# The second network of a macaron block: token tiles in groups of 20 and 12 in place of 16 and 16

## The reference, cut to what matters

```python
def ffn(x):                                   # x: 4096 x 128, 8 experts of hidden width 352
    scores = softmax(x @ gate_w.T)
    sel = top_k(scores + expert_bias, 2)
    # per token: sum over its two experts e, fed with score * x
    #   (silu(xe @ w1[e]) * (xe @ w3[e])) @ w2[e]
x = x + 0.5 * ffn(layernorm(x))               # first network
x = x + attention(layernorm(x))               # 16 heads of width 8, no causal mask
x = x + 0.5 * ffn(layernorm(x))               # second network
```

## Time and profile before

| | us |
|---|---|
| median of three runs | 736.26 |
| the profiled execution | 741.27 |
| its span, first to last instruction | 739.5 |
| first network's loads and routing | about 0 to 237 |
| attention | about 237 to 504 |
| second network's loads | 507 to 688 |
| last 32 result gathers, last sums and stores | 691.65 to 739.5 |

### The profile page before, as it was taken

The page is one execution under the profiler, slowest core; times in us unless marked ns, Lnnn a source line. Parts: engine busy times, 40 slices in busy tenths (PEclk is TensorE's granted clock), DMA queues, the critical chain, the costliest instruction groups (busy, mean ns, idle before and its releaser), DMA issues.

```text
span 739.5 us, 14928 instructions
## 1 busy us (share of the span) xinstructions
PE 622.7 (84%) x5050; PEld 474.7 (64%) x5050; DVE 446.2 (60%) x1164; ACT 390.3 (53%) x912; POOL 302.3 (41%) x312
## 2 busy tenths in 40 slices
PE   6399999999988788999899998898999989999200
PEld 6388899888866334445455554456989979989100
DVE  6956733235456899999999999881576322233111
ACT  1625654445422577777877777773457534444000
POOL 6067614665433273045000010005565057777574
PEclk9999999999999789999999999998999999999655
DMA  8358978887982544445343433035679678887322
GB/s 261 100 164 226 243 219 225 230 249 201 293 235 78 168 143 138 123 137 144 106 149 113 139 107 102 3 111 160 175 221 276 189 194 241 241 256 209 106 78 64
DMA packets 116586, 126.02 MB, mean 170 GB/s; under 512 B 12512, under 2 KB 99168, under 8 KB 116384
## 3 DMA queue, kind: packets, MB, share of 16 engines
q1 hardware_dynamic: 98544, 101.20, 45.6%
q0 software_dynamic: 9088, 18.63, 10.2%
q10 hardware_dynamic: 8880, 5.25, 2.3%
HBM read 89.37 MB, written 35.39 MB: 169 GB/s over the span
## 4 chain that ended last, share of the span: by engine, by line
PE 51%; DVE 24%; DMA 7%; issue 6%; POOL 5%; ACT 4%; SPq 2%; POOLq 0%; ACTq 0%; DVEq 0%
PE banks L684 12%; DVE mx L816 10%; PE banks L656 8%; PE banks L672 8%; PE banks L665 8%; PE banks L1127 4%; POOL rows L588 4%; DMA WR<-in_experts 3%; PE banks L646 2%; PE banks L471 2%; ACT PT L1142 2%; DMA xe<-routed_rows,idx 2%; PE banks L1100 2%; PE banks L1011 2%; DVE resid L803 1%
## 5 line engine op out<-in xcount | busy, mean ns | idle before, releaser
L568 POOL DMA_INDIRECT xe<-routed_rows,idx x156 | 151.0, 968 | 231.5 <-PE banks L646 75.5
L816 DVE TENSOR_REDUCE mx<-banks 128x2 f32<-128x512 f32 x256 | 163.3, 683 | 9.4 <-PE banks L1102 8.1
L1142 ACT ACTIVATE PT<-banks 128x512 f32<-128x512 f32 x256 | 140.5, 603 | 34.5 <-PE banks L1113 32.4
L588 POOL DMA_INDIRECT rows<-slots_out,slot x128 | 123.8, 967 | 69.6 <-issue 27.8
L737 DVE TENSOR_TENSOR hidT<-banks,act 96x256 f32<-96x256 f32 (+1 forms) x92 | 34.9, 380 | 192.3 <-ACT act L718 190.2
L684 PE MATMUL banks<-WR,hidT 128*128 128x128 f32 x936 | 120.6, 276 | 0.6 <-ACT ye L727 0.6
L684 PEld LDWEIGHTS banks<-WR,hidT 128*128 128x128 f32 x936 | 112.6, 192 | 2.9 <-issue 1.0
L656 PE MATMUL banks<-xeT,WR 128*128 128x256 f32 (+1 forms) x368 | 87.0, 359 | 7.2 <-issue 3.0
L672 PE MATMUL banks<-xeT,WR 128*128 128x256 f32 (+1 forms) x368 | 83.7, 350 | 0.0
L665 PE MATMUL banks<-xeT,WR 128*96 128x256 f32 (+1 forms) x368 | 83.2, 349 | 0.0
L1100 PE MATMUL banks<-KS,QS 56*128 56x256 bf16 x256 | 67.9, 283 | 11.6 <-DVE mx L816 9.7
(11 more groups left out here) (160 smaller groups left out, 888.9 us busy)
## 6 DMA issues: line engine op xcount, KB each, us to landing
WR<-in_experts SPq DMA_DIRECT2D x92, 544.0 KB
stacks<-split SPq DMA_DIRECT2D x32, 384.0 KB
slots_out<-ye SPq DMA_DIRECT2D x156, 64.0 KB
QS<-stacks SPq DMA_DIRECT2D x64, 112.0 KB
KS<-stacks SPq DMA_DIRECT2D x64, 112.0 KB
routed_rows<-xn ACTq DMA_DIRECT2D x16, 256.0 KB, 5.1
routed_rows<-xn SPq DMA_DIRECT2D x12, 256.0 KB, 2.3
xe<-routed_rows,idx POOLq DMA_INDIRECT x156, 4.4
```

Of the source, the lines that this page charges most:

```text
L568: eng.indirect_dma_start(xe[:, i % XR, a, :], None, routed_rows[h], bass.IndirectOffsetOnAxis(ap=idx[h][:, tile:tile + 1], axis=0))\
L588: eng.indirect_dma_start(rows[:, k, t, :], None, slots_out[h], bass.IndirectOffsetOnAxis(ap=slot[h][:, k, t:t + 1], axis=0))\
L816: eng.tensor_reduce(mx[:, :, e, pair], maxima_bank(f)[:, :].rearrange("p (q n) -> p q n", q=2), AX.X, ALU.max).then_inc(s_max, 1)
L1142: eng.activation(PT[:, u % 4, 1 - k].rearrange("p t n -> p (t n)"), PS[f % 3], ACT.Exp, scale=scale).then_inc(s_exp2, 1)
```

## The change

`GROUPS = (16, 16, 20, 12)` gives each group its own number of tiles; `FIRST` is its first tile and `LOAD0` its first load. The first network stays at 16 and 16. The second network has 27 + 19 loads in place of 23 + 23; as before 32 pairs and 14 singles. Group 2's loads 21 to 26 are all pairs, and group 3 ends with two singles.

- Routing tensors are sized for 20 tiles and indexed by the group's own size. The constants `count` and the table `there` hold one choice's columns only; `there` is used twice.
- Group 2's routing waits for 10 attention sequences in place of 8. Its statistics have a fifth step. ScalarE and VectorE make 20 tiles of rows each; the fifth block of VectorE lies in two slots of the `xe` ring, which is now `XR` = 11 loads.
- Group 3's routing has tables of its own: `VECTOR_LAST` ends at load 16 where the one before ended at load 19, `SCALAR_LAST` makes the last row by load 15 in place of load 19.
- GpSimd fetches for group 3 from load 21 (3, 2, 2), gathers group 2's 40 results from load 30 (2, 3) beside one fetch a load, and at the end gathers group 3's 24 results in place of 32. The first of these waits for all five sums of group 2, as it reuses their buffers.
- `opening_tensor` has three `keep_pace` products behind each of its five head pairs, 15 in all.

```diff
-XR = 16
+GROUPS = (TH, TH, 20, 12)
+FIRST = (0, TH, 0, GROUPS[2])
+XR = 11
...
-        s_gath = [[sem(f"s_gath{h}_{c}") for c in range(GC)] for h in range(HALVES)]
+        s_gath = [[sem(f"s_gath{g}_{c}") for c in range(t // 4)] for g, t in enumerate(GROUPS)]
...
-            for i in range(KT):
-                if i % (KT // 2) == 0:
-                    eng.wait_ge(s_hot, 6 * g + 3 + 3 * (i // (KT // 2)))
-                last = eng.matmul(PS[7][:, 0:2 * NT].rearrange("p (v j) -> p v j", v=2), hot[:, :, i], brow[:, :, :, i],
-                                  start=i == 0, stop=i == KT - 1)
+            T, K, tiles = GROUPS[g], TOP_K * GROUPS[g], TOP_K * GROUPS[g] + NS
+            for i in range(K):
+                if i % T == 0:
+                    eng.wait_ge(s_hot, 6 * g + 3 + 3 * (i // T))
+                last = eng.matmul(PS[7][:, 0:2 * tiles].rearrange("p (v j) -> p v j", v=2), hot[:, :, i],
+                                  brow[:, :, 0:tiles, i], start=i == 0, stop=i == K - 1)
...
-            for k, c in ((0, 0), (0, 1), (0, 2), (1, 0), (0, 3), (1, 1), (1, 2), (1, 3)):
+            for k, c in ((0, 0), (0, 1), (0, 2), (1, 0), (0, 3), (1, 1), (1, 2), (0, 4), (1, 3), (1, 4)):
...
+        def combined(g, c):
+            return sum(GROUPS[0:g]) // 4 + c + 1
+
+        def combined_before(g, c):
+
+            if 4 * c >= TH:
+                return combined(g, c - TH // 4)
+            return combined(g - 1, max(range(c, GROUPS[g - 1] // 4, TH // 4))) if g > 0 and GROUPS[g - 1] > 4 * c else \
+                combined(g - 2, c) if g > 1 else 0
...
             for pair in range(5):
                 for e in range(2):
                     for _ in largest_scores(eng, (1, pair), e):
...
+                keep_pace(eng, 3, PS[0])
...
-            outs = expert_gpsimd(pool, 2, 6, spread((0, 17, 2)),
-                                 spread((16, NL + 3, 3, 3, 2), (NL + 3, 2 * NL, 1)),
-                                 spread((NL + 3, NL + 15, 1, 1, 2), (NL + 15, 2 * NL, 2)), ((4, 9, 1),))
+            second = LOAD0[3] - NET
+            outs = expert_gpsimd(pool, 2, 6, spread((0, second - 6, 2)),
+                                 spread((second - 6, second + 3, 3, 2, 2), (second + 3, NET, 1)),
+                                 spread((second + 3, NET, 2, 3)), ((4, 9, 1, slice(0, GROUPS[3])),))
...
+        VECTOR_LAST = (1, 1, 1, 2, 16, 0, 4, 4, 16, 3, 3, 3, 2, 2, 1, 19, 1)
+        SCALAR_LAST = (0, 0, 0, 0, 0, 17, 0, 0, 0, 24) + 8 * (4,)
+        TENSOR_LAST = 8 * (0,) + (39,) + 5 * (0,) + (33, 2)
...
-            attention_scalar(act, side, spans((105, 105, 17), (117, 117, 23), (118, 124, 2), (125, 125, 1)))
+            attention_scalar(act, side, spans((105, 105, 17), (117, 117, 23), (118, 126, 2), (127, 127, 1)))
...
-                             (made, spans((124, 124, 1), (125, 125, 2), (126, 126, 1)), None),
+                             (made, spans((124, 124, 1), (125, 126, 2)), None),
...
-                          (done, late(3, 1, 12, 17, 22), -1))
+                          (done, late(3, 1, 9, 13, 17), -1))
```

More of the change, by code:

```diff
@@ L47 @@
 C_STEP = C_REV + EXPERTS
-C_TILE = C_STEP + TH
-C_SEG = C_TILE + NL
-C_PART = C_SEG + EXPERTS * TH
+C_PAIR = C_STEP + TM
+C_SINGLE = C_PAIR + TM
+C_SEG = C_SINGLE + NS
+SEG = {t: C_SEG + EXPERTS * sum(u for u in sorted(set(GROUPS)) if u < t) for t in GROUPS}
+C_PART = C_SEG + EXPERTS * sum(set(GROUPS))
 C_TOK = C_PART + 1
-C_IOTA = C_TOK + KT
+C_IOTA = C_TOK + KM
 C_END = C_IOTA + P
@@ L237, in build, with norm_stats @@
         block = ctx.enter_context(nc.Block())
-        def norm_stats(eng, h, tiles, mean, added=0):
-            for t in range(0, TH, 4):
-                wait(eng, s_add, min(added, 1) * (h * TH + t + 4) // 2)
+        def norm_stats(eng, g, tiles, mean, added=0):
+            for t in range(0, GROUPS[g], 4):
+                wait(eng, s_add, min(added, 1) * (FIRST[g] + t + 4) // 2)
                 for i in range(t, t + 4):
@@ L352, in route_vector @@
                                              ALU.mult, ALU.add))
[L353 removed]
+            link(eng, eng.tensor_tensor(by_e(place), by_e(upto), by_e(taken), ALU.subtract))
             yield
@@ L406, in route_vector @@
+            link(eng, eng.tensor_copy(posb[:, 0:K], pos[:, 0:K]))
             yield
             for c in range(2):
-                part = slice(c * KT // 2, (c + 1) * KT // 2)
-                nk = [P, NT, KT // 2]
-                link(eng, eng.tensor_tensor(there[:, :, part], tileb[:, part].unsqueeze(1).to_broadcast(nk),
-                                            count[:, 0:NT, part], ALU.is_equal))
-                eng.tensor_tensor(brow[:, 0, :, part], there[:, :, part], tokb[:, part].unsqueeze(1).to_broadcast(nk),
+                part = slice(c * T, (c + 1) * T)
+                nk = [P, tiles, T]
+                here = there[:, 0:tiles, 0:T]
+                wait(eng, s_hot, c * (6 * g + 2))
+                link(eng, eng.tensor_tensor(here, tileb[:, part].unsqueeze(1).to_broadcast(nk),
+                                            count[:, 0:tiles, 0:T], ALU.is_equal))
+                eng.tensor_tensor(brow[:, 0, 0:tiles, part], here, tokb[:, part].unsqueeze(1).to_broadcast(nk),
@@ L413, in route_vector @@
                                   ALU.mult).then_inc(s_hot, 1)
-                eng.tensor_scalar(brow[:, 1, :, part], there[:, :, part], CT[:, C_PART:C_PART + 1], None,
+                eng.tensor_scalar(brow[:, 1, 0:tiles, part], here, CT[:, C_PART:C_PART + 1], None,
                                   ALU.mult).then_inc(s_hot, 1)
                 yield
-                eng.tensor_tensor(hot[:, :, part], posb[:, part].unsqueeze(1).to_broadcast([P, P, KT // 2]),
-                                  count[:, :, part], ALU.is_equal).then_inc(s_hot, 1)
+                eng.tensor_tensor(hot[:, :, part], posb[:, part].unsqueeze(1).to_broadcast([P, P, T]),
+                                  count[:, :, 0:T], ALU.is_equal).then_inc(s_hot, 1)
@@ L419, in route_vector @@
                 yield
-            for first, last, end in ((0, NP, last_pair), (NP, NL, last_single)):
-                ne = [P, last - first, EXPERTS]
-                link(eng, eng.tensor_tensor(passed[:, first:last, :],
-                                            CT[:, C_TILE + first:C_TILE + last].unsqueeze(2).to_broadcast(ne),
+            for first, many, numbers, end in ((0, T, C_PAIR, last_pair), (T, NS, C_SINGLE, last_single)):
+                ne = [P, many, EXPERTS]
+                link(eng, eng.tensor_tensor(passed[:, first:first + many, :],
+                                            CT[:, numbers:numbers + many].unsqueeze(2).to_broadcast(ne),
@@ L539, in root_gpsimd @@
             eng.tensor_tensor(rough[h][:, t], var[h][:, t], half_power[:, t], ALU.pow).then_inc(s_pow, 1)
-        def load_of(i):
-            g, j = i // NL, i % NL
-            if j % 3 == 2:
-                return g, NP + j // 3, 1, (2 * NP + j // 3) * P
-            l = j - (j + 1) // 3
-            return g, l, 2, 2 * l * P
+        orders = []
+        for pairs in GROUPS:
+            order, single = [], 0
+            for j in range(pairs + NS):
+                pair = j - single
+                if pair == pairs or j % 3 == 2 and single < NS:
+                    order.append((pairs + single, 1, (2 * pairs + single) * P))
+                    single += 1
+                else:
+                    order.append((pair, 2, 2 * pair * P))
+            orders.append(order)
+        def load_of(i):
+            g = max(g for g in range(len(GROUPS)) if LOAD0[g] <= i)
+            return g, *orders[g][i - LOAD0[g]]
         def landed(i):
@@ L573, in gathers_out @@
         def gathers_out(eng, g):
-            for n in range(KT):
+            for n in range(TOP_K * GROUPS[g]):
                 gather_out(eng, g, n)
@@ L601, in combine @@
         def combine(eng, g, h):
-            for c in range(GC):
+            for c in range(GROUPS[g] // 4):
                 combine_part(eng, g, h, c)
```

368 lines of the change are left out of this document (190 added, 178 removed).

## The result

| | before | after |
|---|---|---|
| time, median (range) | 736.33 (735.81 to 742.08, 4 runs) | 748.78 (746.79 to 750.65, 4 runs) |
| ratio to before | | 1.0123, 95% interval 1.0081 to 1.0166 |
| profiled execution's span | 739.5 | 746.6 |
| mean granted clock | 0.946 | 0.941 |

The prediction is wrong, and its range (727 to 740.5) does not hold the time. The two profiles differ by 7.1 us. Where medians are compared, the ratio is taken within one set.

A forecast was written before the change was run, and what follows sets the result against it. VectorE and TensorE bound attention, TensorE the second network, GpSimd's gathers the tail. Load 21: -1.5 + 3.5 + 6.4 + 0.3 - 1.2 = 7.5 us later; after GpSimd's tail, 738.1 against 739.5, so 736.26 - 1.4 = 734.9, range 727 to 740.5.

The forecast's parts named there:

- The opening: Start of attention: 15 constant products hold TensorE's clock, a gain of 1.5 us, between a gain of 3 and a loss of 1.
- VectorE's growth: Attention's side work for 20 tiles (statistics, small instructions, tables): 3.5 us later at the index products, ends 1.5 and 7.
- The index products: Group 2's eight more on TensorE: 1.2 us if the weight load sets 0.15 each, 2.4 if moved columns count.
- The hand-over: Attention to second network: ScalarE's last two rows behind `onT`, then three stores, put the first fetch 6.4 us later.
- the base: Median of the kernel before, 736.26 us, from which the forecast took off 1.4 us.
- The clock after the hand-over: Start of the second network: low TensorE clock after a wait of some 6 us, 0.3 us added.
- The tables lose their rate: Rival, group 2's routing tables in attention: new strides halve VectorE's rate, 5.6 us more, 740.5 us; chance 0.15.
- The tail gains in full: Rival, first fetch to end: the first fetch slips by far less than 6.4 us, giving 729.2 us; chance 0.25.
- The gathers do not back up: Rival, GpSimd from load 30: 50 issues run faster or start earlier, end of span 732.6 us; chance 0.15.
- the chance of 0.08 on slower: Whole kernel: chance 0.08 of a time over 743.6 us, slower by one per cent.
- the ring: GpSimd's fetches: a ring of 11 loads costs nothing, as the order keeps GpSimd at most 11 loads ahead.

The follow-up runs named there:

- c_tail_order: Changed kernel with group 3's result gathers, sums and output stores in chunk order 2, 3, 1: 741.94 us without two far-off runs, ratio 1.0038.
- a_rows_early: Changed kernel with ScalarE's last four rows of group 2 all made at pair 125, ahead of the last probabilities: 739.72 us, ratio 0.9984.
- c_table_turned: Changed kernel with its row table laid out so that index products read it without gaps and VectorE writes it at gaps: 768.32 us, one run.
- a_idx_early: Changed kernel with the first 16 of group 2's 40 index products one attention step earlier: 746.06 us, ratio 1.0088.
- a_no_products: Changed kernel without the 15 constant products in the opening of attention: 749.38 us, ratio 1.010.
- b_both_early: Changed kernel with ScalarE's last four rows early and 16 index products one attention step earlier: 738.26 us, ratio 0.9972.
- b_rows_late: Kernel before, 16 tiles in group 2, with its last rows on ScalarE made later, one of them behind `onT`: 748.56 us, ratio 1.0121.
- d_sync_after: Changed kernel with the store of ScalarE's last four rows put behind VectorE's last two on SyncE: 747.13 us, ratio 1.0116.

## Why the prediction was wrong

Its chain of events was right from end to end, but its sizes ahead of the first fetch were not, and for the index products it also had the wrong cause. It had the first fetch near 509; it came at 517.57, 8.5 us later. Behind that the working holds: load 21 was 7.9 us later than predicted (606.42, said 598.5), and the end of the span 8.5 (746.6, said 738.1). So the whole error in the span lies ahead of the first fetch, in the sizes of these terms of the sum:

- **The opening: a gain of 1.5.** The sum behind sequence 2 is at 282.72, 2.2 us later than before. The clock held in 240 to 250 and fell twice after it. Off by 3.7 in this profile. But profiles of programs that agree up to there differ by more (c_tail_order has that sum at 280.22, a_rows_early at 286.06), so one execution can't size this term. What all profiles show is the fall that moved: in the ten with the products (c_table_turned aside) the clock in 268 to 276 is 0.59 to 0.84, in the six without 0.79 to 1.00. The step counted what the full clock saves in 245 to 250 and not what a later fall costs.
- **VectorE's growth: 3.5.** From the sum at 282.72 to the one at 485.73 it grew by 3.0 (480.55 and 280.56 in before), from there to the products by 2.4: 5.4, inside the bounds of 1.5 to 7. The 2.4 repeats: 13.7 to 14.1 us in all six profiles that have the larger tables and the products where after has them, 11.7 in four of before's six (12.6 and 14.1 in two whose clock stood at 0.80 and 0.61 in 490 to 495). The 3.0 does not: that stretch is 198.6 to 203.0 us in the six kernels built on before and 200.0 to 205.9 in the ten built on after (c_table_turned, with its slow writes, aside), 1.6 apart in the mean. The tables are as worked out, 0.65, 0.65, 0.70 and 1.48; what I may have put too low is not shown; it could be the small instructions or the fifth step of statistics. Off by 1.9 between these two profiles, by some 0.5 in the mean of all.
- **The index products: 1.2, at most 2.4.** Measured 3.2, above the high end. This is the step whose mechanism was wrong: it took the weight load to set the 0.15. In c_table_turned a whole product, its weight load beside it, takes 0.079, so the read of the table is what counts: 2.0 us for wider products at a wider distance, and 1.2 for eight more. Even "by columns" was too little, because the layout moved the elements from 64 to 80 bytes apart, which the step did not look at. Off by 2.0. The Trainium skill ("SBUF — State Buffer", section "Door 1: The DMA port swizzle") says that reads that cross into a new line of 16 bytes each time pay a penalty; that spaced reads cost two and a half times the dense ones here (0.20 and 0.079) agrees. It would have pointed at the moved operand; that 80 bytes cost more than 64 does not follow from it.
- **The hand-over: 6.4.** The rows behind `onT`, the three stores and the fetch stand as forecast, and `onT` follows the products by the same 3.5 us as before. From `onT` to the fetch it is 6.16 us, in place of 507.1 - 501.9 = 5.2: three stores in flight at once land 2.3, 2.9 and 3.2 us after issue, the last of them is the one that counts, and it left 0.95 behind the first and not 0.74. Off by 1.0.

3.7 + 1.9 + 2.0 + 1.0 = 8.6, the 8.5 but for rounding. Of these the 2.0 repeats from profile to profile, and the 1.0 nearly (`onT` to fetch is 6.2 in a_idx_early and c_tail_order, 7.8 in a_no_products); the 3.7, and 1.4 of the 1.9, lie within what single executions differ by. The other 5 us of the miss are the base: the profile lay 5 us over the median of three runs, and I took the difference off that median. Over 88 more runs of before it is 738 to 740, so the base was low by 2 to 4.

- **The clock after the hand-over: 0.3.** Too little. The first turn's products run at half clock (2.05 us, 0.54 granted in 520 to 530), and turn to end is 224.4 where it is 221.8 in a_rows_early, whose clock is 0.82 and then 1.00 in 510 to 530: 2.6 us. The rule of the Trainium skill that I weighed ("TensorE: Matmul & The Clock Gate", section "Part 1: The HAM clock gate"), a throttled start after a pause, was the better guide for this wait of 5.4 us; the waits of 1.16 us in before and 1.20 in b_both_early were followed by products of 1.10 us, at the full clock, so not every pause does it. What hid part of the miss: from the first fetch to the first turn it is 4.6 us, in before 6.6.
- **The rivals.** The tables lose their rate (0.15): refuted. The tail gains in full (0.25): it is what the kernel does when the rows are early, in so far as turn to end falls to 221.8; but the first turn at 518 uses up the gain, and the time is that of before. The gathers do not back up (0.15): they did, as forecast. (The 732.6 given for this rival is an end of the span, where the others are in time; in time it would be 729.4.) No rival had the right side by the right way; the chance of 0.08 on slower was too small for a hand-over of which each term had a high end that I left unused.

What the change costs, then, by runs: the last rows on ScalarE behind `onT`, 9 us in after and 10 in before; the larger group's tables, index products and small work, up to 8.6 us ahead of the first turn (5.4 and 3.2; 5.6 of it repeats), which the shorter last group gives back behind it; the ring, nothing; the 15 constant products, nothing that shows. In b_rows_late the first turn is 6.6 us later and the span 7.7, yet the medians differ by 10: the profiled execution of before (741.27) lay 2.8 us above the median of that set, 738.5, and that of b_rows_late (749.03) 0.5 above its own.

## What to carry to other kernels

Before a group grows, find the last instruction on each in-order engine that its first consumer needs, and place it ahead of whatever that engine waits for; a half-microsecond row behind a copy that waits for TensorE, with three ready stores queued behind its own, cost 10 us. Stores that are ready go ahead of a store that is not, on the same queue. When a layout's stride changes, price every reader of it by distance and count, above all the moved operand of a narrow product.

## What the runs showed of the hardware that was not expected

- A bf16 product with a moved operand read at a distance: 62 columns at 80 bytes 0.148 us (8 in 1.18), 78 at 64 bytes 0.152, 78 at 80 bytes 0.165 to 0.171, 94 at 80 bytes 0.201, and 78 or 94 without gaps 0.079. Granted clocks of 0.98 and 0.50 make no difference to the 94.
- VectorE writing 940 bf16 elements at a distance of 188 bytes takes 4.7 and 5.0 us; without gaps it takes 0.65 and 0.70.
- Fifteen cheap products held the clock at 1.00 in the ten microseconds at which they were aimed, and it fell to 0.57 in the eight behind. In all ten profiles with them (c_table_turned aside) it is 1.00 in 240 to 250, and in 268 to 276 it is 0.59 to 0.84; in the six without, 0.50 to 0.67 in 245 to 250 and 0.79 to 1.00 in 268 to 276. No time to the next sum shows a gain.
- The same instructions up to there, and the sum behind sequence 2 begins at 280.02 (d_sync_after), 280.22, 282.72 (after) and 286.06 (a_rows_early). A single profile shows the order of causes and the length of waits; it does not measure an edit of 2 us.
